# A pre-norm attention and gated-FFN layer on one core: row products moved out of the stacked chunks

## What is computed

```python
q, k, v = proj(Wq, bq), proj(Wk, bk), proj(Wv, bv)      # of layernorm(x); (B, 16, 512, 8)
idx = clip(pos[None, :] - pos[:, None], -20, 20) + 20
attn1 = einsum('bhqd,bhkd->bhqk', q, k)
attn2 = einsum('bhqd,qkd->bhqk', q, rel_k[idx])
attn = softmax((attn1 + attn2) / sqrt(8), axis=-1)
w1 = einsum('bhqk,bhkd->bhqd', attn, v)
w2 = einsum('bhqk,qkd->bhqd', attn, rel_v[idx])
x = x + (w1 + w2).reshape(B, S, E) @ Wo.T + bo
x = x + (silu(n(x) @ Wg.T) * (n(x) @ Wu.T)) @ Wd.T       # n = layernorm; weights / 127
```

## Time and profile before

| what | value |
|---|---|
| median of three runs | 1368.93 us |
| the profiled execution | 1367.64 us, span 1365.9 us |
| PE busy in the span | 1260.8 us (92%) |
| DVE busy | 918.4 us (67%) |
| ACT busy | 758.0 us (55%) |
| POOL busy | 571.7 us (42%) |
| mean granted clock of PE | 0.973 |

### The profile page before, as it was taken

The page is one execution under the profiler, slowest core; times in us unless marked ns, Lnnn a source line. Parts: engine busy times, 40 slices in busy tenths (PEclk is TensorE's granted clock), DMA queues, the critical chain, the costliest instruction groups (busy, mean ns, idle before and its releaser), DMA issues. The chain is left out here.

```text
span 1365.9 us, 67623 instructions
## 1 busy us (share of the span) xinstructions
PE 1260.8 (92%) x30680; PEld 936.6 (69%) x30688; DVE 918.4 (67%) x1780; ACT 758.0 (55%) x1413; POOL 571.7 (42%) x1047
## 2 busy tenths in 40 slices
PE   4388589999999999999999999999999999979998
PEld 3256257777777777777777777777777777756766
DVE  5378867767677777676766767677767676146664
ACT  4388256656566666565665656566656565523332
POOL 5397435353434444443435343434444343122221
PEclk9799679999999999999999999999999999989999
DMA  4455310211120111102020111021110100113231
GB/s 129 134 202 200 108 46 9 56 29 46 30 55 25 50 41 33 49 27 55 19 55 25 50 31 55 21 54 36 38 48 27 53 22 9 41 41 93 70 93 47
DMA packets 101542, 76.99 MB, mean 56 GB/s; under 512 B 13256, under 2 KB 97032, under 8 KB 101256
## 3 DMA queue, kind: packets, MB, share of 16 engines
q1 hardware_dynamic: 101256, 72.67, 18.1%
HBM read 44.86 MB, written 26.21 MB: 52 GB/s over the span
## 5 line engine op out<-in xcount | busy, mean ns | idle before, releaser
L1046 DVE TENSOR_REDUCE b_mx<-b_a 128x1 f32<-128x512 f32 x1024 | 658.6, 685 | 233.1 <-PE b_a L813 227.7
L1007 ACT ACTIVATE b_p<-b_s 128x512 f32<-128x512 f32 x1024 | 569.8, 595 | 399.3 <-PE b_s L854 313.3
L904 PE MATMUL b_pv<-b_p,vg 128*16 128x128 f32 x8192 | 287.0, 275 | 0.1
L777 POOL TENSOR_TENSOR qd<-q,one 48x512 bf16<-48x512 bf16 x256 | 266.7, 1042 | 27.7 <-POOL b_np L759 5.1
L854 PE MATMUL b_s<-qd,z 112*128 112x32 bf16 (+1 forms) x6016 | 248.5, 189 | 0.1
L754 POOL TENSOR_TENSOR b_np<-b_db,one 128x16 bf16<-128x16 bf16 x192 | 39.3, 266 | 470.4 <-DVE b_mx L1046 467.2
L813 PE MATMUL b_a<-k,q 48*128 48x512 bf16 x1024 | 202.8, 393 | 27.0 <-DVE b_mx L1046 11.5
L854 PEld LDWEIGHTS b_s<-qd,z 112*128 112x128 bf16 x6016 | 205.8, 99 | 10.1 <-issue 0.2
L904 PEld LDWEIGHTS b_pv<-b_p,vg 128*16 128x16 f32 x8192 | 196.3, 96 | 21.4 <-issue 0.4
L839 PE MATMUL b_s<-q,k 54*128 54x64 bf16 (+3 forms) x4608 | 188.2, 201 | 5.7 <-issue 2.5
L839 PEld LDWEIGHTS b_s<-q,k 54*128 54x128 bf16 (+1 forms) x4608 | 126.6, 95 | 91.4 <-PE b_s L839 29.2
(11 more groups left out here) (125 smaller groups left out, 1237.1 us busy)
## 6 DMA issues: line engine op xcount, KB each, us to landing
x<-in_x SPq DMA_DIRECT2D x32, 256.0 KB, 3.3
scratch_qop<-a_parts SPq DMA_DIRECT2D x16, 384.0 KB, 2.5
scratch_kop<-a_parts SPq DMA_DIRECT2D x16, 384.0 KB, 3.1
k<-scratch_kop SPq DMA_DIRECT2D x32, 192.0 KB
q<-scratch_qop SPq DMA_DIRECT2D x32, 192.0 KB
scratch_v<-a_vr SPq DMA_DIRECT2D x16, 256.0 KB, 3.2
k<-scratch_kop SPq DMA_DIRECT2D x32, 128.0 KB
q<-scratch_qop SPq DMA_DIRECT2D x32, 128.0 KB
```

Of the source, the lines that this page charges most:

```text
L777: nc.gpsimd.tensor_tensor(dst, src, one, ALU.mult).then_inc(s["qd_ready"], 1)
L904: nc.tensor.matmul(PV[32 * a:32 * a + V16, g * P:(g + 1) * P], v[:, 0 if t <= i else 1, t, h, :], PR[at.c % 2][:, t, h, :], start=(t == 0 ...
L1007: nc.scalar.activation(out, src, ACT.Exp, scale=SCALE).then_inc(s["p_ready"], 1)
L1046: nc.vector.tensor_reduce(MX[v.c % 2][:, h:h + 1], PA[(n + hp) % NBANK][:, :], AX_X, ALU.max, negate=True).then_inc(s["a_used"], 1)
```

## The change

Units 1 to 61 are affected. The list `order` stays as it is: the pairs keep their numbers and their banks. What changes is where they stand. `SPOTS[i]` lists the eight chunks that hold the pairs of a unit of block i: no pair in the two stacked chunks (2i and 2i+1), one in each of the six others, and a second one in the two chunks that `DOUBLE[i]` names: 2 and 4 for i=0, 1 and 4 for i=1, 1 and 2 for i=2 and for i=3. A second pair stands at the end of its chunk, behind the filler. Unit 0 is as before. On DVE the second pair's maxima come behind `keep_values` in chunk 1 and ahead of `normalise` in chunk 3.

```diff
--- before.py
+++ after.py
@@ -628,10 +628,16 @@
             order.append((u + LEAD, hh))
     place = {pair: n for n, pair in enumerate(order)}
 
-    def pairs_beside(at, c):
+    DOUBLE = ((2, 4), (1, 4), (1, 2), (1, 2))
+    SPOTS = [sorted([c for c in range(SUB) if c // NG != i] + list(DOUBLE[i])) for i in range(T)]
+
+    def pairs_beside(at, c, second=False):
 
         u = at.count()
-        return [(1, EARLY + c)] * (u == 0 and c < HH - EARLY) + [(u + LEAD, c)] * (u + LEAD < U)
+        if u == 0:
+            return [] if second else [(1, EARLY + c)] * (c < HH - EARLY) + [(LEAD, c)]
+        here = [(u + LEAD, hh) for hh in range(HH) if SPOTS[u % T][hh] == c and u + LEAD < U]
+        return here[1:] if second else here[:1]
 
     def window(t, i):
         return abs(t - i) <= 1
@@ -813,9 +819,9 @@
                     nc.tensor.matmul(PA[(n + hp) % NBANK][:, :], Q[p][r, hh, hp, i * P:(i + 1) * P], K[p][r, hh, :],
                                      start=True, stop=True).then_inc(s["a_ready"], 1)
 
-            def row_pairs_ahead(at, c):
-
-                for u, hh in pairs_beside(at, c):
+            def row_pairs_ahead(at, c, second=False):
+
+                for u, hh in pairs_beside(at, c, second):
                     row_pair(at.plus(u - at.count()), hh)
 
             def head_scores(at, c, hp, n, opens):
@@ -976,6 +982,7 @@
                         value_products(at, 1, range(H // NQ4)[2 * (c - 5):2 * (c - 4)])
                     if c == 7:
                         value_products(at, 2)
+                    row_pairs_ahead(at, c, True)
 
             run_all(unit, PER, U)
             end = at0(U - 1)
@@ -1076,6 +1083,9 @@
                     if before.exists():
                         if c == 1:
                             keep_values(before)
+                    for u, hh in pairs_beside(at, c, True):
+                        row_max(at.plus(u - at.count()), hh)
+                    if before.exists():
                         if c == 3:
                             normalise(before)
```

## The result

The changed kernel takes 1453.74 us (median of 4, 1452.01 to 1457.69) beside 1368.98 us for the kernel before on the same chip (1364.98 to 1370.85). The ratio is 1.0628, 95% interval 1.0607 to 1.065. That is 84.8 us slower; the forecast was +86.2 us on 1368.93, 1455 us.

What follows compares the result with a forecast made beforehand. PE was taken as the bound, busy 945.84 of 970 us. Second pairs' work plus stalls less relief gave +1.56, +0.72, +1.68, +1.74 per unit (i=0 to 3), +86.2 us in all: 1455 us, range 1440 to 1468.

Steps and rivals of the forecast that it cites:

- The main step: On PE, a pair following a second pair stalls for that one's first maximum: 106 stalls of 0.81 to 1.26 us.
- The distance in window chunks: Second pair to the next window chunk's pair: 1.16 us, 1.49 with the masking; stalls 0.81 and 1.14 us.
- The distance in plain chunks: Second pair to the next plain chunk's pair: 1.16 us, 1.49 with the masking; stalls 0.93 and 1.26 us.
- The relief: Pairs gone from stacked chunks save PE 0.41 us behind output transposes, 0.32 elsewhere; 0.32 to 0.73 per unit.
- Units with i=1: Each of 16 units gains +0.72 us: 0.23 work plus 0.81 stall less 0.32 relief.
- The work of the second pair: At the chunk's end it holds PE for 0.23 us, seven times per batch; the eighth (i=1, chunk 1) costs nothing.
- the free place inside a window chunk: A pair there costs PE nothing, filling the wait for `half`: L839 to L854 takes 0.58 us with or without it.
- rival b: DVE falls behind after a double, so third pairs wait too: +32 us, 1487 us; chance 0.04.
- rival c: PE's clock falls to the 1.2 GHz level with stalls of about 1 us: about 1540 us; chance 0.04.
- rival d: The next pair finds its wait already met, so only work counts: 1354.5 us, faster; chance 0.02.

Runs made afterwards that it cites:

- The removal alone: Changed kernel with the second pairs' row products and maxima left out, a constant for their bound: 1327.9 us, ratio 0.9726 to the kernel before.

## Why the prediction was right, and where its terms were off

- **The main step held**: the second pair stands too close to the next one, and each pair waits for the first maximum of its forerunner. 106 waits were forecast and 106 are there. Shortening the maximum by 0.40 us shortened all four distances by 0.40. The waits' list has 89.0 us, not the "about 100" of the prediction, because it counts from the modelled end of a matmul; by the distances the stalls are 102 us.
- **The distance in window chunks**, 1.16 forecast, is 1.17; with the masking 1.49 forecast, 1.48 read.
- **The distance in plain chunks** was under-sized: 1.16 forecast, 1.26 read, and 1.57 instead of 1.49 with the masking. The chain was taken from places with one wait, and here the matmul has two; the experiment with the pair ahead of the `p_ready` wait closes the gap. 45 places, about 4 us.
- **The relief** was under-sized for one kind of removal. Behind the guard transpose (one per i=1 unit) it is 0.42 us, not 0.32 (the pairless chunk starts 0.09 after L941, the pair stood 0.19 after L935), as the range had allowed. For the others, 0.32 and 0.41 were right: the traces have 0.32 to 0.33 and 0.42. The removal alone measured 37.8 us (34 to 41) where its trace has 42.6 between undisturbed fillers. The idle times without a releaser differ from one execution to the next; what causes them is open.
- **Units with i=1**, read in the same way, cost 1.03 us at chunk 4 (1.92 to 2.96 from filler to filler) and give back 0.43 at the guard transpose: 0.61 us instead of 0.72, and the difference is the relief just named. Their time alone came out at 0.46 (0.24 to 0.58 by the interval). 0.61 is just above that; the two profiled executions differ by 10.8 us, 0.68 per unit. The idle times, 0.3 to 1.0 us each in these units, blur both.
- **The work of the second pair**, 0.23 us, and the free place inside a window chunk are as forecast (804.15 to 804.38).
- **DVE's backlog** (rival b) did not come: the pair after a double has no wait in the waits' list (106, no more). **The clock** (rival c) stayed at 1.00 with 109.6 us of idle time, 89.0 of it in 106 pieces of 0.7 to 1.3 us, so what the Trainium skill describes in "TensorE: Matmul & The Clock Gate", section "A second HAM failure mode: psum-queue depth-cycling", did not happen here. **The other side** (rival d) would have needed stalls under 0.14 us; they average about 0.96.
- The total came close (84.8 against 86.2) in part because two errors of its terms cancel. Undisturbed units of the changed kernel are longer by 1.65 (i=0), 0.61 (i=1), 1.63 (i=2) and 1.82 us (i=3), where 1.56, 0.72, 1.68 and 1.74 were forecast: 4 us more for the plain distances, about 2 less for the guard transpose, and the rest less in small differences, mostly of i=3.

## What to carry to other kernels

With three banks and two taken at a time, the distance between two uses counts, not how many lie in a stretch: check it on both sides of the place to which a step is moved. A consumer that is busy for only 71% of a stretch (DVE, 688 of 970 us) can still cost 6% if its work comes in pairs. Before moving work out of a full stretch, look for a wait in the stretch that the same work could fill, and see if it isn't inside the wait already.

## What the runs showed of the hardware that I had not expected

- A matmul that waits for two semaphores starts 0.09 us later than one that waits for one, though the second had been raised before (1.26 us against 1.17 in 15 places, 1.57 against 1.48 in 15 more); 0.051 us of it is an extra instruction of PE's sequencer.
- TensorE kept the 2.4 GHz level through 106 stalls of about 1 us, at 90% busy time.
- A full-height product follows the guard transpose after 0.09 us, a half-height one after 0.18 to 0.19; behind the value products both take 1.00 us.
